# Rows and results in Pool's order at the start of the second experts

## The chip, the cores and the metric

One NeuronCore of one Trainium2 chip runs the whole program in one launch. The metric is the device time of that launch in microseconds. Engines are called PE (TensorE), DVE (VectorE), ACT (ScalarE), Pool (GpSimd) and SP (SyncE); L12 is line 12 of the kernel before.

## The reference

`x` holds 128 graphs of 64 nodes with 128 features, 8192 tokens in all, and runs through four residual stages. The change touches the seam between the last two:

```
x = x + gnn0(layernorm(x), adj)       # graph attention
x = x + ffn0(layernorm(x))            # 8 experts, top 2, relu
x = x + gnn1(layernorm(x), adj)       # three GRU layers on each graph
x = x + ffn1(layernorm(x))            # 16 experts, top 2

# ffn1, for every token
logits = x @ gate_w + gate_b
top_probs, top_idx = top_k(softmax(logits), 2)
hidden = silu(x @ w1[e]) * (x @ w2[e])
out = sum over the two experts e of top_prob[e] * (hidden @ w3[e])
```

All of it is computed in float32; the counting of ranks in the routing uses bfloat16 zeros and ones.

## The kernel before

The tokens are cut into 16 groups (`NG`) of 4 tiles of 128 tokens. The two expert stages compute only what is routed. For each group and each of the two chosen experts, a token has a slot in a queue in HBM (`queue1`), in which the tokens of an expert lie together. A *row send* is one indirect DMA that Pool issues at L429: it scatters 128 normalised tokens with their ids to their slots; a group needs TOPK * G = 8 of them (`queue_rows`). Group s uses buffer s % 4 of `c.rows` and the four semaphores `c.landed[s % 4]`.

The experts then read the queue in 144 tiles, two at a time, in 72 *pairs*. Which tiles can be known before the last groups are counted, the first `KNOWN` = 80 tiles or 40 pairs, come first; a table of the rest is written later. The function `experts` with layer = 1 is this stage. A step k of it does for each engine what belongs to three pairs at once (`steps`, `body`):

- SP loads the pair's tiles into `xq` (4 buffers), after the ids of four pairs before have been copied out.
- PE turns pair k (`ps_x`, L2326), does the up matmuls of pair k - 2 (16 of 128 x 128 into `e_ps_h`, two buffers, L2338) and the down matmuls of pair k - 4 (8, into `e_ps_y`, L2352).
- DVE copies pair k's ids into `y_ids` (8 buffers, L2432), copies the two experts' up weights into `e_up_of` (L2434), and multiplies the gate into `e_hT` for pair k - 2 (L2486). Ahead of the ids copy it waits until the results of pair k - 8, which used the same buffer, have landed.
- ACT copies the turned pair, does the silu (`e_gate`, L2409) and copies the results of pair k - 4 into `y_rows` (L2413).
- Pool sends the results of pair k - 4: two indirect DMAs at L2291 that scatter 128 results each to HBM. The first waits for `y_copied`. The second also waits for `h_made`, the up matmuls of the pair three further on.

The order on each engine is written by hand. Work of the stage before, on its last groups, is put between the steps by `between(k)`, called after step k: the statistics, the routing and the rows of groups 14 and 15 (`last`), and DVE's table of the remaining tiles behind steps 12 to 15. Groups 12 and 13 (`even`, `odd`) are ready as the stage begins: Pool sends their last 12 rows in front of its steps, with `rstd_and_shift` of groups 14 and 15 (L294, L296) among them. The rows of group 14 are sent all at once behind Pool's step 5, those of group 15 behind step 7.

Steps 0 to 15 (two rounds of `UNROLL` = 8) are straight code, steps 16 to 39 and the later ones are loops on the engine.

The results' first halves (t = 0) count on `c.landed[0]` and `c.landed[1]` (L2200), which groups 12 and 13 (s % 4 = 0 and 1) count on as well; the second halves count on `c.sent`. So Pool waits, ahead of its steps, until the rows of groups 12 and 13 have landed. SP waits ahead of pair 40 for the rows of groups 14 and 15.

Behind the last pair follows `finish`: SP loads the results back, ACT and DVE weight them and add them to `x`, SP stores `out`.

## Time and profile before

| what | value |
|---|---|
| median of three runs | 1069.83 us (1068.66 to 1069.91) |
| the profiled execution's own time | 1068.49 us |
| its span in the trace | 1066.8 us |
| PE busy | 950.5 us, 89% |
| DVE busy | 765.3 us, 72% |
| Pool busy | 589.0 us, 55% |
| ACT busy | 553.6 us, 52% |

The second experts take about the last quarter of the span. In the page's 40 slices of 26.7 us, PE's row reads 9 in nearly all slices and lower in those around 780 to 850 us, where one stage passes into the next. A timeline has one line for an instruction or a run of like ones: start, length, engine, line, operation and, in brackets, how long the engine had been idle and what ended that. A list of waits sums these. Windows give busy times of a stretch with the clock granted to PE (1.00 is 2.4 GHz, 0.50 is 1.2 GHz).

### The profile page before, as it was taken

The numbers are of one execution on the slowest core, as the hardware profiler recorded it, in microseconds if no ns is written. First come the engines' busy times: TensorE is split into PE (matmuls) and PEld (weight loads), VectorE is DVE, ScalarE is ACT, GpSimd is POOL, SyncE is SP. The second block draws the span as 40 slices with busy tenths as digits, with TensorE's granted clock in tenths as the row PEclk, the third lists the DMA queues.
The fourth block names the chain that finished last, engine by engine and source line by source line (L and its number), as shares of the span: only waits on it lengthen the run. The fifth ranks groups of instructions, "written<-read, shape, count | busy, mean of one in ns | idle before, by whom it ended". The sixth has DMA issues, their size and how long they took to land. (4 is left out here: it accounts for less than half of the span.)

```text
span 1066.8 us, 24109 instructions
## 1 busy us (share of the span) xinstructions
PE 950.5 (89%) x6368; PEld 772.8 (72%) x6369; DVE 765.3 (72%) x2973; ACT 553.6 (52%) x1359; POOL 589.0 (55%) x623
## 2 busy tenths in 40 slices
PE   4676999999999996899999999999969499999960
PEld 3566999999989996456555555555559499999960
DVE  5567888888876665478898899988866265555548
ACT  4655655665553342355576565655544144444455
POOL 2155677777777754001446455554546777676660
PEclk9656999999999999899999999999989799999985
DMA  9612422222222422210303303130115244333359
GB/s 225 225 38 59 103 76 83 76 79 75 76 83 74 123 66 82 80 53 27 97 23 109 100 26 107 35 122 26 36 45 116 67 116 119 86 94 92 86 206 313
DMA packets 101516, 99.41 MB, mean 93 GB/s; under 512 B 32412, under 2 KB 86300, under 8 KB 101148
## 3 DMA queue, kind: packets, MB, share of 16 engines
q1 hardware_dynamic: 84252, 62.83, 21.6%
q0 software_dynamic: 17152, 35.29, 9.9%
q8 instruction: 46, 0.75, 0.3%
q14 instruction: 66, 0.54, 0.2%
HBM read 55.44 MB, written 42.62 MB: 92 GB/s over the span
## 5 line engine op out<-in xcount | busy, mean ns | idle before, releaser
L429 POOL DMA_INDIRECT queue<-rows,slots x256 | 258.1, 1008 | 161.5 <-issue 72.5
L2291 POOL DMA_INDIRECT result<-y_rows,y_ids x144 | 143.3, 995 | 62.5 <-issue 52.6
L1015 POOL DMA_INDIRECT result<-y_rows,y_ids x136 | 134.8, 991 | 62.6 <-issue 36.1
L2338 PE MATMUL e_ps_h<-e_xT,e_up_of 128*128 128x128 f32 x1152 | 146.2, 282 | 15.3 <-DVE e_hT L2486 15.3
L2338 PEld LDWEIGHTS e_ps_h<-e_xT,e_up_of 128*128 128x128 f32 x1152 | 139.6, 198 | 16.0 <-issue 15.8
L1562 PEld LDWEIGHTS a_ps_y<-w_sb,a_hT 128*128 128x128 f32 x1088 | 131.2, 192 | 4.1 <-issue 1.3
L1562 PE MATMUL a_ps_y<-w_sb,a_hT 128*128 x1088 | 132.6, 275 | 1.1 <-DVE y_rows L1174 1.1
L1546 PE MATMUL a_ps_up<-a_xT,a_up_of 128*128 128x256 f32 x448 | 106.8, 381 | 0.3 <-issue 0.3
L2486 DVE TENSOR_TENSOR e_hT<-e_ps_h,e_gate 128x512 f32<-128x512 f32 x72 | 49.6, 689 | 72.4 <-ACT e_gate L2409 72.1
L2409 ACT ACTIVATE e_gate<-e_ps_h 128x512 f32<-128x512 f32 x72 | 43.0, 597 | 109.5 <-PE e_ps_h L2338 109.5
L1546 PEld LDWEIGHTS a_ps_up<-a_xT,a_up_of 128*128 128x128 f32 x448 | 80.7, 190 | 10.6 <-issue 0.5
L2014 ACT ACTIVATE g_rg<-g_ps_r,g_bsum 128x512 f32<-128x512 f32 x48 | 32.9, 685 | 92.8 <-PE g_ps_n L1931 92.8
L2352 PE MATMUL e_ps_y<-w_sb,e_hT 128*128 x576 | 78.5, 281 | 1.8 <-ACT y_rows L2413 1.8
L1374 ACT ACTIVATE a_hT<-a_ps_up,b_sb 128x256 f32<-128x256 f32 (+1 forms) x160 | 60.2, 436 | 35.0 <-PE a_ps_up L1546 23.4
L294 POOL TENSOR_TENSOR head_rstd<-head_vare,half_neg 128x4 f32<-128x4 f32 x15 | 15.7, 1046 | 107.5 <-DVE head_vare L287 107.5
L2352 PEld LDWEIGHTS e_ps_y<-w_sb,e_hT 128*128 128x128 f32 x576 | 72.3, 197 | 2.1 <-issue 2.1
L2434 DVE COPY e_up_of<-w_sb 128x512 f32 x144 | 60.2, 457 | 1.3 <-issue 0.4
L1155 DVE TENSOR_SCALAR a_hT<-a_ps_up,b_sb 128x256 f32<-128x256 f32 x112 | 48.9, 477 | 7.9 <-PE a_ps_up L1546 7.0
L1366 ACT ACTIVATE a_xT<-a_ps_x 128x256 f32<-128x256 f32 x68 | 25.8, 379 | 54.7 <-PE a_ps_x L1533 54.7
L2083 DVE SCALAR_TENSOR_TENSOR g_cand<-g_ps_hn,b_hh_sb,g_rg 128x512 f32<-128x512 f32 x48 | 35.8, 745 | 20.2 <-ACT g_rg L2014 19.9
L1924 PE MATMUL g_ps_r<-g_state,w_hh_sb 128*128 128x512 f32 x96 | 49.4, 596 | 0.0
L1929 PE MATMUL g_ps_r<-g_agg,w_agg 128*128 128x512 f32 x96 | 49.0, 592 | 0.0
(307 smaller groups left out, 2069.1 us busy)
## 6 DMA issues: line engine op xcount, KB each, us to landing
xq<-queue SPq DMA_DIRECT2D x168, 64.5 KB
g_y<-result SPq DMA_DIRECT2D x20, 512.0 KB, 4.3
xq<-queue SPq DMA_DIRECT2D x56, 129.0 KB
result<-y_rows,y_ids POOLq DMA_INDIRECT x280, 2.3
x_res<-x SPq DMA_DIRECT2D x16, 256.0 KB, 3.9
w_sb<-w SPq DMA_DIRECT2D x2, 2048.0 KB, 11.7
queue<-rows,slots POOLq DMA_INDIRECT x256, 2.4
w_sb<-w SPq DMA_DIRECT2D x16, 256.0 KB, 4.1
```

Of the source, the lines that this page charges most:

```text
L429: pool.indirect_dma_start(out=queue, out_offset=bass.IndirectOffsetOnAxis(ap=c.slots[q][:, k, t:t + 1], axis=0), in_=c.rows[q][:, k, t, :] ...
L1015: pool.indirect_dma_start(out=c.result0, out_offset=bass.IndirectOffsetOnAxis(ap=ids[slot.k][:, t, :].bitcast(U32), axis=0), in_=y[slot.k] ...
L1374: last = act.activation(hT[slot.b][:, q * size:(q + 1) * size], ps_up[0][:, q * size:(q + 1) * size], ACT.Relu, bias=up_b[:, bass.ds(exper ...
L1546: last = pe.matmul(ps_up[half][:, q * DOUBLE:(q + 1) * DOUBLE], up_of[b][:, (2 * half + q) * P:(2 * half + q + 1) * P], xT[b][:], start=Tr ...
L1562: last = pe.matmul(ps_y[:, t * D:(t + 1) * D], hT[at_down.b][:, first:first + P], down[:, bass.ds(expert_of(at_down, t) * wide + q * P, P) ...
L1924: pe.matmul(ps_r[:], c.w_hh[:, 0:D], h[:], start=True, stop=False)
L1929: pe.matmul(ps_r[:], c.w_agg[:, l, 0:D], agg[b][:], start=False, stop=True)
L2291: pool.indirect_dma_start(out=result, out_offset=bass.IndirectOffsetOnAxis(ap=ids[at_down.k][:, t, :].bitcast(U32), axis=0), in_=y[at_down ...
L2338: last = pe.matmul(ps_h[b][:, t, q * P:(q + 1) * P], up_of[at_up.k % 4][:, t, q * P:(q + 1) * P], xT[at_up.k % 4][:, t, :], start=True, st ...
L2352: last = pe.matmul(ps_y[:, t * D:(t + 1) * D], hT[at_down.k % 4][:, t, q * P:(q + 1) * P], down[:, bass.ds(e * (chunks * P) + q * P, P)], ...
L2434: last = v.tensor_copy(up_of[now.k % 4][:, t, :], up[:, bass.ds(expert_of(0, t) * wide, wide)])
L2486: v.tensor_tensor(hT[at_up.k % 4][:], ps_h[at_up.k % 2][:, :, H1:2 * H1], gate[at_up.k % 2][:], ALU.mult).then_inc(hT_vec, 1)
```

## The change

The results' first halves count on `c.sent_first`, eight semaphores that the first experts use and the rows don't. Pool no longer waits for the rows of groups 12 and 13; SP waits for them ahead of pair 40, with the others. The 16 rows of groups 14 and 15 are sent one at a time: `rows_by` spreads them over 24 steps, two for every three, behind the results of steps 6, 7, 9, 10 and so on to 28. For this all 40 steps with known tiles are straight code on Pool; the other engines keep their two rounds and their loops. And of the 12 rows in front of the steps three instead of two come before the first `rstd_and_shift`.

```diff
-        sent = [[c.landed[k // SPREAD][k % SPREAD] for k in range(UNROLL)], c.sent]
-        before = [[c.landed_before[k // SPREAD][k % SPREAD] for k in range(UNROLL)], c.sent_before[:]]
+        sent = [c.sent_first, c.sent]
+        before = [c.first_sent[:], c.sent_before[:]]
...
-            for i in range(2):
+            for i in range(rounds):
                 for k in range(UNROLL):
                     step(i, k)
                     if between:
                         between(i * UNROLL + k)
-            with eng.Fori(2, known // UNROLL) as i:
-                for k in range(UNROLL):
-                    step(i, k)
+            if rounds < known // UNROLL:
+                with eng.Fori(rounds, known // UNROLL) as i:
+                    for k in range(UNROLL):
+                        step(i, k)
...
                     for q in range(TURN):
-                        if q >= 2:
-                            wait_landed(sp, c, q, 0)
+                        wait_landed(sp, c, q, 0)
...
+            each_group = TOPK * G
+            shared_slots = 24
+            rows_by = [min(max(k - 5, 0) * PAIR * each_group // shared_slots, PAIR * each_group) for k in range(known + 1)]
+
             def between(k):
-                if k == 5:
-                    rows_of(last[0])
-                if k == 7:
-                    rows_of(last[1])
+                for row in range(rows_by[k], rows_by[k + 1]):
+                    rows_of(last[row // each_group], row % each_group, row % each_group + 1)
 
             even, odd = (At(NG // 2 - 2, b) for b in range(2))
-            rows_of(even, 4, 6)
+            rows_of(even, 4, 7)
             rstd_and_shift(pool, c, tail.norm, tail.VT, tail.GT, tail.AT0, last[0])
-            rows_of(even, 6, 8)
+            rows_of(even, 7, 8)
             rows_of(odd, 0, 2)
             rstd_and_shift(pool, c, tail.norm, tail.VT, tail.GT, tail.AT0, last[1])
             rows_of(odd, 2, 8)
-            for q in range(2):
-                wait_landed(pool, c, q, 0)
-            steps(pool, body, between=between)
+            steps(pool, body, between=between, rounds=known // UNROLL)
```

Pool's order at the start of the second experts, before (`queue` are row sends, `result` are result sends, two to a pair; x4 means four in a row):

```order
-L429 DMA queue<-rows,slots 135168x129 x2
-L294 TENSOR_TENSOR l_tail_rstd<-l_tail_vare,half_neg 128x4
-L296 TENSOR_TENSOR l_tail_shift<-l_tail_minus_mean,l_tail_rstd 128x4
-L429 DMA queue<-rows,slots 135168x129 x4
-L294 TENSOR_TENSOR l_tail_rstd<-l_tail_vare,half_neg 128x4
-L296 TENSOR_TENSOR l_tail_shift<-l_tail_minus_mean,l_tail_rstd 128x4
-L429 DMA queue<-rows,slots 135168x129 x6
-L2291 DMA result<-y_rows,y_ids 20480x128 x4
-L429 DMA queue<-rows,slots 135168x129 x8
-L2291 DMA result<-y_rows,y_ids 20480x128 x4
-L429 DMA queue<-rows,slots 135168x129 x8
-L2291 DMA result<-y_rows,y_ids 20480x128 x16
```

And now:

```order
+L429 DMA queue<-rows,slots 135168x129 x3
+L294 TENSOR_TENSOR l_tail_rstd<-l_tail_vare,half_neg 128x4
+L296 TENSOR_TENSOR l_tail_shift<-l_tail_minus_mean,l_tail_rstd 128x4
+L429 DMA queue<-rows,slots 135168x129 x3
+L294 TENSOR_TENSOR l_tail_rstd<-l_tail_vare,half_neg 128x4
+L296 TENSOR_TENSOR l_tail_shift<-l_tail_minus_mean,l_tail_rstd 128x4
+L429 DMA queue<-rows,slots 135168x129 x6
+L2291 DMA result<-y_rows,y_ids 20480x128 x6
+L429 DMA queue<-rows,slots 135168x129
+L2291 DMA result<-y_rows,y_ids 20480x128 x2
+L429 DMA queue<-rows,slots 135168x129
+L2291 DMA result<-y_rows,y_ids 20480x128 x4
```

The 16 row sends of groups 14 and 15 stood in two runs of eight, behind pair 1 and behind pair 3; now one stands behind pair 2 (six results), one behind pair 3, one behind pair 5, and so on. One row has moved ahead of the first `rstd`.

SP's order ahead of the load of pair 40, with its waits:

```order
 L600 ISA
 L600 DMA xq<-queue 128x129
-L590 TENSOR_LOAD tile_row [waits landed2_3,landed3_0,landed2_2,landed3_1,landed2_1,landed3_2,landed2_0,landed3_3,t1_written,t1_padded]
+L590 TENSOR_LOAD tile_row [waits landed1_3,landed2_0,landed1_2,landed2_1,landed1_1,landed2_2,landed1_0,landed2_3,landed0_3,landed3_0,landed0_2,landed3_1,landed0_1,landed3_2,landed0_0,landed3_3,t1_written,t1_padded]
 L600 ISA [waits e1_ids_copied]
 L600 DMA xq<-queue 128x129
```

The semaphores of buffers 0 and 1 (groups 12 and 13) have joined those of 2 and 3. No instruction of SP, PE, ACT or DVE has moved otherwise.

## Rows read from the trace of the kernel before

**Rows 1.** The page: the span, and PE's busy time and share.
```profile
span 1066.8 us, 24109 instructions
...
PE 950.5 (89%) x6368; PEld 772.8 (72%) x6369; DVE 765.3 (72%) x2973; ACT 553.6 (52%) x1359; POOL 589.0 (55%) x623
```

**Rows 2.** Waits, 795 to 870 us: engine, line, releaser; total, times, longest in us.
```profile
DVE y_ids L2432 <- DMA result<-y_rows,y_ids: 24.9, 5, 10.7
...
PE e_ps_h L2338 <- DVE e_hT L2486: 15.3, 2, 7.8
```

**Rows 3.** Timeline of PE: start, length, line, operation, count, [idle before it <- releaser].
```profile
822.91 1.95 PE L2338 MATMUL e_ps_h<-e_xT,e_up_of 128*128 128x128 f32 x16
...
836.66 3.58 PE L2338 MATMUL e_ps_h<-e_xT,e_up_of 128*128 128x128 f32 x16 [7.79 <-DVE e_hT L2486]
...
841.19 1.95 PE L2338 MATMUL e_ps_h<-e_xT,e_up_of 128*128 128x128 f32 x16
...
851.81 3.76 PE L2338 MATMUL e_ps_h<-e_xT,e_up_of 128*128 128x128 f32 x16 [7.56 <-DVE e_hT L2486]
...
857.25 1.95 PE L2338 MATMUL e_ps_h<-e_xT,e_up_of 128*128 128x128 f32 x16
...
915.36 1.95 PE L2338 MATMUL e_ps_h<-e_xT,e_up_of 128*128 128x128 f32 x16
```

**Rows 4.** Windows of 5 us: length, PE busy, granted PEclk, DMA share, GB/s.
```profile
825.00:830.00 5.00, 3.87 (x35) 1.00 0.21 65
835.00:840.00 5.00, 3.34 (x16) 0.51 0.35 97
```

**Rows 5.** Timeline of Pool, from the last rows of group 13 on.
```profile
809.77 0.95 POOL L429 DMA_INDIRECT queue<-rows,slots  x1 [0.30 <-issue]
814.82 0.96 POOL L2291 DMA_INDIRECT result<-y_rows,y_ids  x1 [4.09 <-issue]
817.46 0.96 POOL L2291 DMA_INDIRECT result<-y_rows,y_ids  x1 [1.69 <-ACT y_rows L2413]
...
830.07 0.96 POOL L429 DMA_INDIRECT queue<-rows,slots  x1 [0.30 <-issue]
831.34 0.96 POOL L2291 DMA_INDIRECT result<-y_rows,y_ids  x1 [0.31 <-issue]
832.60 0.96 POOL L2291 DMA_INDIRECT result<-y_rows,y_ids  x1 [0.30 <-issue]
...
847.75 0.96 POOL L2291 DMA_INDIRECT result<-y_rows,y_ids  x1 [0.30 <-issue]
```

**Rows 6.** Timeline of DVE behind the first long wait.
```profile
834.95 0.17 DVE L2432 COPY y_ids<-xq 128x2 f32<-128x2 f32 x1 [10.68 <-DMA result<-y_rows,y_ids]
...
835.83 0.68 DVE L2486 TENSOR_TENSOR e_hT<-e_ps_h,e_gate 128x512 f32<-128x512 f32 x1
```

**Rows 7.** Pool: a window (length, busy, count, PE's clock, DMA), and its longest distance.
```profile
863.10:890.50 27.40, 20.93 (x21) 1.00 0.45 124
...
869.73 1.19 POOL L2291 DMA_INDIRECT result<-y_rows,y_ids  x1 [0.30 <-issue]
871.22 0.95 POOL L2291 DMA_INDIRECT result<-y_rows,y_ids  x1 [0.30 <-issue]
```

**Rows 8.** Timeline at the stage's start: Pool's two rstd, ACT's first results.
```profile
793.85 1.27 POOL L294 TENSOR_TENSOR l_tail_rstd<-l_tail_vare,half_neg 128x4 f32<-128x4 f32 x1 [1.59 <-DVE l_tail_vare L287]
...
801.25 1.11 POOL L294 TENSOR_TENSOR l_tail_rstd<-l_tail_vare,half_neg 128x4 f32<-128x4 f32 x1
...
805.05 0.43 ACT L2413 ACTIVATE y_rows<-e_ps_y 128x128 f32<-128x128 f32 x2
```

**Rows 9.** Tile `queue`, Pool, 785 to 860 us: who waited for its sends (us, times).
```profile
  POOL result L2291: 4.1, 1
```

**Rows 10.** Timeline of ACT: its last results, at the stage's end.
```profile
1032.94 0.45 ACT L2413 ACTIVATE y_rows<-e_ps_y 128x128 f32<-128x128 f32 x2 [2.47 <-PE e_ps_y L2352]
```

**Rows 11.** Line L2434, 863 to 890 us: least, median, most ns of one.
```profile
L2434 DVE COPY e_up_of<-w_sb x21: 407/427/658, 863.3 to 889.7; 128x512 f32 x21
```

More of the change, by code:

```diff
@@ L2199, in experts, with steps @@
         y_made, y_copied = sem("y_made"), sem("y_copied")
-        sent = [[c.landed[k // SPREAD][k % SPREAD] for k in range(UNROLL)], c.sent]
-        before = [[c.landed_before[k // SPREAD][k % SPREAD] for k in range(UNROLL)], c.sent_before[:]]
+        sent = [c.sent_first, c.sent]
+        before = [c.first_sent[:], c.sent_before[:]]
         sent_of = [16 * (pairs // UNROLL + (k < pairs % UNROLL)) for k in range(UNROLL)]
-        def steps(eng, body, first_word=0, words=0, between=None):
+        def steps(eng, body, first_word=0, words=0, between=None, rounds=2):
             held = []
@@ L2293, in body, with rows_of @@
                             in_=y[at_down.k][:, t, :], in_offset=None).then_inc(sent[t][at_down.k], 16)
-            def rows_of(at, first=0, most=TOPK * G):
+            def rows_of(at, first, most):
                 wait(pool, tail.VK, "slots", at.s)
@@ L2494, in _ @@
                 finish.sum(v)
-    for k in range(UNROLL):
-        c.landed_before[k // SPREAD][k % SPREAD] += sent_of[k]
-        c.sent_before[k] += sent_of[k]
 def combine(v, c, y, t, k, g):
```

## The prediction

> **What bounds the kernel now.** I read the page first: PE is busy 950.5 of 1066.8 us [rows 1], so a change in the second experts pays only where PE stands still there. The list of waits for 795 to 870 us names one cause [rows 2]: DVE waited five times, 24.9 us in all, for result transfers to land before it could reuse a slot's ids buffer (L2432), and PE waited twice, 15.3 us in all, for DVE's `e_hT` behind that. Call U(p) the time at which PE starts the up matmuls of pair p (L2338). The timeline gives U(8) = 822.91, U(10) = 836.66, U(11) = 841.19, U(12) = 851.81, U(13) = 857.25 and U(33) = 915.36 [rows 3]. From U(13) to U(33) are 20 pairs in 58.1 us, 2.90 us each: PE without a break, at its own pace. From U(8) to U(33) are 25 pairs in 92.45 us, where 25 x 2.90 = 72.5: 20 us are lost. They lie in the steps to U(10) (13.75 instead of 5.8), U(11) (4.53), U(12) (10.62) and U(13) (5.44, each instead of 2.9): 8.0 + 1.6 + 7.7 + 2.5 = 19.8. The 1.6 and the 2.5 are matmuls at a lower clock after each stop: the 16 up matmuls take 3.58 and 3.76 us instead of 1.95 [rows 3], and the granted clock of 835 to 840 us is 0.51, the 1.2 GHz level [rows 4].
>
> Pool's timeline tells why [rows 5]. Pool sends the results of pairs 0 and 1, then eight rows of group 14 up to 830.07, then pair 2 at 831.34 and 832.60. The rows of group 15 stand in the same way between pairs 3 and 4; pair 4's second result goes at 847.75. Pair p+8 needs pair p's landing. From the start of pair 2's second result to U(10) are 4.06 us, from pair 4's to U(12) 4.06 us again. In it lie the landing (DVE's copy starts 2.35 us after), the two up copies and the product [rows 6]. So **U(p+8) = start of pair p's second result + 4.06**, or U(p+7) + 2.90, whichever is later.
>
> **The change, part by part.**
>
> *Removed bursts.* With no eight rows in front of any pair both stops go, with the slow matmuls behind them: up to 20 us. What is late next has to be worked out, since the 16 rows don't vanish: they are spread as two rows per three slots, behind pairs 2, 3, 5, 6 and so on to 23 and 24.
>
> *Pool's own pace.* With DVE mostly waiting, Pool made 13 starts from 831.34 to 847.75 [rows 5], 1.262 us from start to start. With PE and DVE at full pace, from 863.1 to 890.5 us, it made 21 in 27.4 us, 1.30 [rows 7]. The second fits the new stretch, since DVE will be working; I take 1.30 and keep 1.262 as the good end. A slot needs 2 + 2/3 sends: 3.47 us against PE's 2.90. Over the 24 slots Pool needs 13.6 us more than PE. It starts with a lead; that is used up, and then PE waits for Pool.
>
> *Where Pool starts.* Now it waits for the landing of groups 12 and 13, whose semaphores the results share: the last row goes at 809.77, the first result at 814.82, after 4.09 us of idle time, and the second at 817.46 after 1.69 us more [rows 5]; one result send waited 4.1 us for a row send [rows 9]. With semaphores of their own the results need only `y_rows`, which ACT has written for pair 0 at 805.05 [rows 8]. The third row ahead of the first `rstd` fits in Pool's 1.59 us of waiting for `vare` [rows 8], and one row less then stands ahead of the second `rstd`: it comes about 1.26 us earlier than 801.25, and so does ACT's normalising behind it. The last of the twelve rows thus starts near 808.5 and pair 0's first result near 809.8. The 1.69 us has no cause that the trace shows: its row names an ACT copy, but by the order of ACT's copies that is pair 3's, and this result waits for pair 0's; if it stays, the start counts as 811.5. This is the other end that I keep.
>
> *The sum.* Pair 2's second result, five starts on, goes at 816.3, and PE at its own pace would need it at 822.91 + 5.8 - 4.06 = 824.65: the lead is 8.3 us. From the first result to the second of pair 25 are 51 starts of results and 16 of rows, 67 in all. 809.8 + 67 x 1.30 = 896.9; plus 4.06 is U(33) = 901.0. Pair 25 is the right one to ask, as the last with all 16 rows in front; behind it Pool needs 2.60 us per pair and PE sets the pace again. PE alone would be at 822.91 + 72.5 = 895.4, so it waits about 5.6 us in all, in pieces of 0.7 to 1.0 us over the last ten or so of the pairs up to 33. Before, U(33) was 915.36. **The gain is 14.4 us.** The ends: 67 x 1.262 gives 898.4, a gain of 17.0; with the 1.69 us it is 902.7, a gain of 12.7.
>
> *Hidden parts, at nothing.* SP waits before pair 40 for all rows, also those of groups 12 and 13. The last row starts at 809.8 + 65 x 1.30 = 894.3 and has landed by 896.7; SP gets there only after DVE has copied the ids of pair 36, just ahead of U(34), near 903.7. That is 7 us of cover; a row landing later than that would delay the load of pair 40, and the loads queued behind it on SP, one for one. Queued behind the new rows on Pool are only results, which the sum holds. Pool runs 24 more slots as straight code instead of a loop: it does without the register work of the loop, and the 16 straight slots of before ran on at 1.26 us. PE's and ACT's orders don't change. The 1.26 us by which the second `rstd` comes earlier shortens a PE wait early on, but Pool sets U(33), not PE, so it is worth nothing.
>
> *From U(33) to the end* both kernels are alike: PE at 2.90 us per pair, then ACT's last results, which wait for PE [rows 10], and the finish behind them. So the gain reaches the end whole. The profiled run took 1068.49 us, its span was 1066.8; it would be 1054.1. The median of three is 1.3 us above it, and from that I forecast 1069.83 - 14.4 = **1055.4 us**.
>
> **A rule weighed.** Pool's send of 0.96 us became up to 1.19 us where DVE worked, with 1.49 us between two starts at worst [rows 7], and the mean rose by only 0.04 us. The Trainium skill, "SBUF — State Buffer", section "Who interferes with whom", says that a DVE copy in a 2-port mode and GpSimd exclude each other for a whole instruction, so that descriptors of a Pool transfer can't be written meanwhile. By that rule the change would be worse than its count of sends, as it puts more sends beside running copies; the trace agrees with a small effect at most. What full exclusion gives, worked out from rows, is the last rival below.
>
> **The rivals.**
>
> *Pool starts no earlier* (the change doesn't do what its semaphores are for). If the 4.09 us was not the landing, the first result is at 813.5 or so: 813.5 + 67 x 1.262 to 1.30 + 4.06 is U(33) = 902.1 to 904.7, a gain of 10.7 to 13.3: 1056.5 to 1059.1 us. For it speaks the unexplained 1.69 us beside it; against it [rows 9], though the timeline has only "issue" for it. 12%.
>
> *The clock falls in the short waits.* A fall cost 1.6 or 2.5 us in the two stops. Once PE is late by this it no longer waits for Pool until Pool has used up the time again, so falls don't add up: one lies on the path, so the gain is 14.4 or 12.7 less 1.6 to 2.5 us, 10.2 to 12.8: 1057.0 to 1059.6 us. Against it: from 825 to 830 PE was busy 3.87 of 5 us and was granted 1.00, the 2.4 GHz level [rows 4]. 8%.
>
> *Pool isn't in the way.* If its lead lasts, PE sets the pace: gain 20, 1049.9 us. That needs less than 1.22 us from start to start, which no stretch of sends has. 4%.
>
> *Pool starves, and the kernel is slower.* DVE's two up copies of a slot take 0.427 us each at full pace [rows 11]. If each held Pool for its whole time, 24 slots add 24 x 0.854 = 20.5 us to 64 sends, so 1.262 + 0.32 = 1.58 us from start to start: U(33) = 809.8 + 105.9 + 4.06 = 919.8, slower by 4.4, 1074.2 us. It decides from 1.515 us on, where 67 sends eat the whole gain; at the worst single distance of 1.49 the gain is 1.7 us. Against it: 21 sends in a row beside full DVE work took 1.30. 5%, split between a small gain, nothing, and slower.
>
> **How the numbers follow.** The forecast case (gain 12.7 to 17.0) has 71%, the rivals 12, 8, 4 and 5. The range reaches from the good end, 1052.8 less the 0.8 us or so between runs, 1052.0, to the bad end of the first two rivals, 1060.0. About 0.2% (2 us) is what a measurement of this kernel can tell from no change; all cases but the starved Pool are beyond it on the fast side: faster 0.95, same 0.02, slower 0.03.
>
> **What would show it.** In the changed profile: the first result near 809.8 (811.5 if the odd gap stays); rows single between results; the row of PE's waits for `e_hT` with 5 us in short pieces instead of 15.3 us in two, and all of them late; DVE's waits for landings in the same slots; U(33) near 901; granted clock 1.00 from 830 to 1000 us; 1.30 us between Pool's starts. The forecast fails if Pool's distance passes 1.33 us (each 0.03 us is 2 us), or if another transfer, such as the load of pair 40, ends later than a result.

## The result and the profile after

| | before | changed |
|---|---|---|
| median of four runs each, same chip | 1069.31 us (1068.66 to 1069.91) | 1052.2 us (1051.91 to 1053.0) |
| the profiled execution, its span | 1068.49, 1066.8 us | 1051.91, 1050.2 us |

The changed kernel takes 0.9841 of the time before (95% interval 0.9824 to 0.9858), 17.1 us less. The forecast was 1055.4 us, a gain of 14.4; the profiled executions differ by 16.6. On the third chip of the experiments below it took 1052.37 us beside 1069.65, a ratio of 0.9848 (0.9828 to 0.9867).

The page of the changed kernel, its first two lines, answers to [rows 1]. PE makes as many matmuls as before in 16.6 us less; it is busy 6.3 us less, having fewer matmuls at the lower clock:

```profile
span 1050.2 us, 24044 instructions
...
PE 944.2 (90%) x6368; PEld 764.4 (73%) x6369; DVE 764.9 (73%) x2973; ACT 554.1 (53%) x1359; POOL 589.1 (56%) x623
```

The list of waits, 795 to 905 us (who waited for what: us in total, times, longest), answers to [rows 2]:

```profile
DVE y_ids L2432 <- DMA result<-y_rows,y_ids: 31.2, 19, 4.4
...
PE e_ps_h L2338 <- DVE e_hT L2486: 4.8, 7, 1.1
```

DVE waits longer in all than before, but in 19 pieces, and PE's 15.3 us in two stops have become 4.8 us in seven pieces of at most 1.1 us.

PE's timeline answers to [rows 3] (start, length, line, operation; in brackets the idle time and what ended it). These are the up matmuls of pairs 8, 18, 33 and 71:

```profile
820.04 1.95 PE L2338 MATMUL e_ps_h<-e_xT,e_up_of 128*128 128x128 f32 x16
...
850.27 2.02 PE L2338 MATMUL e_ps_h<-e_xT,e_up_of 128*128 128x128 f32 x16 [1.08 <-DVE e_hT L2486]
...
899.61 1.58 PE L2338 MATMUL e_ps_h<-e_xT,e_up_of 128*128 128x128 f32 x12
...
1009.43 1.95 PE L2338 MATMUL e_ps_h<-e_xT,e_up_of 128*128 128x128 f32 x16
```

From U(8) to U(17) PE keeps its 2.90 us per pair; the first up matmuls behind a wait are pair 18's. U(33) is at 899.61, where 901.0 was forecast and 915.36 was before.

Windows of PE (stretch, its length, busy time, granted clock, DMA share, GB/s) answer to [rows 4]:

```profile
825.00:850.00 25.00, 24.19 (x218) 1.00 0.35 98
850.00:900.00 50.00, 45.87 (x393) 1.00 0.41 109
900.00:1000.00 100.00, 100.00 (x899) 1.00 0.34 95
```

The clock stays at its 2.4 GHz level through the short waits. Pool's timeline answers to [rows 5]: the last of the twelve rows, the results of pairs 0 to 2 without a gap (three of the six are shown), the first row of group 14, and 76 us later the last row of group 15 and pair 25's results:

```profile
807.86 0.95 POOL L429 DMA_INDIRECT queue<-rows,slots  x1 [0.30 <-issue]
809.12 0.96 POOL L2291 DMA_INDIRECT result<-y_rows,y_ids  x1 [0.30 <-issue]
810.38 0.95 POOL L2291 DMA_INDIRECT result<-y_rows,y_ids  x1 [0.31 <-issue]
...
815.44 0.96 POOL L2291 DMA_INDIRECT result<-y_rows,y_ids  x1 [0.31 <-issue]
816.70 0.96 POOL L429 DMA_INDIRECT queue<-rows,slots  x1 [0.30 <-issue]
...
892.87 0.96 POOL L429 DMA_INDIRECT queue<-rows,slots  x1 [0.30 <-ACT y_rows L2413]
894.13 0.96 POOL L2291 DMA_INDIRECT result<-y_rows,y_ids  x1 [0.31 <-issue]
895.40 0.96 POOL L2291 DMA_INDIRECT result<-y_rows,y_ids  x1 [0.30 <-issue]
```

**Where the 16.6 us are.** Up to U(33) 915.36 - 899.61 = 15.75. From U(33) to U(71) both kernels take 109.8 us. From U(71) to ACT's last results behind the last down matmuls, before took 1032.94 - 1025.17 = 7.77 us and the changed kernel 1016.38 - 1009.43 = 6.95: 0.8 more. Behind that both take 33.8 or 33.9 us. The 0.8 us is a matter of clock. These are PE's last down matmuls and ACT's last results, first of before, then of the changed kernel:

```profile
1030.94 1.97 PE L2352 MATMUL e_ps_y<-w_sb,e_hT 128*128 x8 [0.95 <-ACT y_rows L2413]
```

```profile
1015.19 1.15 PE L2352 MATMUL e_ps_y<-w_sb,e_hT 128*128 x8 [0.95 <-ACT y_rows L2413]
```

```profile
1016.38 0.45 ACT L2413 ACTIVATE y_rows<-e_ps_y 128x128 f32<-128x128 f32 x2 [1.66 <-PE e_ps_y L2352]
```

Same work, same wait of 0.95 us in front, 1.97 us against 1.15. Windows of PE over these matmuls, of before and of the changed kernel:

```profile
1031.00:1033.00 2.00, 1.91 (x8) 0.52 1.03 404
```

```profile
1015.00:1017.00 2.00, 1.15 (x8) 1.00 1.02 401
```

Before was granted 0.52, the 1.2 GHz level, the changed kernel 1.00. No instruction of the change is there. But the slow last matmuls are in the other kernel below that sends its rows in bursts as well (own semaphores alone: 2.00 us, and 41.6 us from U(71) to the end of the span, as in before), and in none of the eleven profiles without bursts (40.8 us). So it may be chance, or it may follow from the bursts; no run tells which.

### The profile page after: what moved, and what is told of

Read it like the earlier page. It is cut to its first block and busy times, and to the rows that moved or that the text cites. A ratio compares the mean times of both kernels' runs of the same rounds, so it can differ in the third digit from the quotient of the medians.

```text
span 1050.2 us, 24044 instructions
## 1 busy us (share of the span) xinstructions
PE 944.2 (90%) x6368; PEld 764.4 (73%) x6369; DVE 764.9 (73%) x2973; ACT 554.1 (53%) x1359; POOL 589.1 (56%) x623
## 5 line engine op out<-in xcount | busy, mean ns | idle before, releaser
L2338 PE MATMUL e_ps_h<-e_xT,e_up_of 128*128 128x128 f32 x1152 | 142.4, 277 | 4.9 <-DVE e_hT L2486 4.8
L2338 PEld LDWEIGHTS e_ps_h<-e_xT,e_up_of 128*128 128x128 f32 x1152 | 135.6, 193 | 6.9 <-DVE e_hT L2486 3.0
L2352 PE MATMUL e_ps_y<-w_sb,e_hT 128*128 x576 | 76.3, 275 | 1.8 <-ACT y_rows L2413 1.8
L2352 PEld LDWEIGHTS e_ps_y<-w_sb,e_hT 128*128 128x128 f32 x576 | 70.1, 192 | 2.1 <-issue 2.1
L2434 DVE COPY e_up_of<-w_sb 128x512 f32 x144 | 60.1, 457 | 2.5 <-issue 0.2
## 6 DMA issues: line engine op xcount, KB each, us to landing
w_sb<-w SPq DMA_DIRECT2D x2, 2048.0 KB, 12.6
```

The costliest lines, as they stand in the source:

```text
L2338: last = pe.matmul(ps_h[b][:, t, q * P:(q + 1) * P], up_of[at_up.k % 4][:, t, q * P:(q + 1) * P], xT[at_up.k % 4][:, t, :], start=True, st ...
L2352: last = pe.matmul(ps_y[:, t * D:(t + 1) * D], hT[at_down.k % 4][:, t, q * P:(q + 1) * P], down[:, bass.ds(e * (chunks * P) + q * P, P)], ...
L2434: last = v.tensor_copy(up_of[now.k % 4][:, t, :], up[:, bass.ds(expert_of(0, t) * wide, wide)])
```

## Experiments

Where the program before the second experts ends varies: Pool's first row send of this stage starts between 789.4 and 792.0 us in the profiled executions of all kernels here. So times inside the stage are given as distances from that send (789.42 in the changed kernel, 789.92 in before), where the changed kernel on two chips differs by 0.07 us at U(33). "First" and "second" are pair 0's two result sends, "pair 2" is pair 2's second result. "Less than before" is the median beside the before run on the same chip (1069.31, 1068.65, 1069.55 or 1069.65 us).

| kernel | first, second | pair 2 | U(8) | U(33) | U(37) | median, us | less than before | ratio (95%) |
|---|---|---|---|---|---|---|---|---|
| before | 24.89, 27.54 | 42.68 | 32.99 | 125.43 | 137.03 | | | |
| changed | 19.70, 20.96 | 26.02 | 30.62 | 110.19 | 121.86 | 1052.20 | 17.1 | .9841 (.9824 to .9858) |
| changed, third chip | 19.64, 20.90 | 25.97 | 30.57 | 110.12 | 121.79 | 1052.37 | 17.3 | .9848 (.9828 to .9867) |
| own semaphores alone | 19.66, 20.93 | 36.18 | 30.58 | 118.83 | 130.42 | 1062.13 | 6.5 | .9928 (.9909 to .9948) |
| spread rows alone | 25.89, 28.53 | 33.59 | 32.60 | 117.61 | 129.28 | 1061.87 | 6.8 | .9940 (.9924 to .9955) |
| 12 slots | 19.67, 20.93 | 27.25 | 30.59 | 114.33 | 125.92 | 1057.79 | 10.9 | .9903 (.9888 to .9918) |
| 28 slots | 19.68, 21.23 | 26.28 | 30.75 | 107.52 | 120.86 | 1052.17 | 16.5 | .9846 (.9831 to .9860) |
| two rows first | 21.15, 22.41 | 27.45 | 31.93 | 111.51 | 123.18 | 1052.57 | 17.0 | .9841 (.9822 to .9860) |
| four rows early | 15.10, 18.89 | 24.19 | 30.58 | 109.22 | 120.88 | 1051.57 | 18.0 | .9832 (.9815 to .9848) |
| four early, 28 slots | 15.09, 18.88 | 25.41 | 30.57 | 106.26 | 118.84 | 1050.25 | 19.3 | .9817 (.9798 to .9835) |
| the same, third chip | 15.11, 18.89 | 25.43 | 30.58 | 106.05 | 119.01 | 1050.36 | 19.3 | .9826 (.9806 to .9846) |
| two early, 28 slots | 17.12, 18.88 | 25.42 | 30.57 | 106.56 | 119.02 | 1050.81 | 18.8 | .9829 (.9809 to .9849) |
| up copies as maximum | 19.47, 20.73 | 26.68 | 30.90 | 113.98 | 125.65 | 1055.73 | 13.8 | .9868 (.9848 to .9888) |

### The two halves of the change

*Own semaphores alone*: the rows of groups 14 and 15 go in bursts of eight behind steps 5 and 7, as before, and Pool keeps its loop from step 16 on. The third row ahead of the first `rstd` stays.

```diff
             def between(k):
-                for row in range(rows_by[k], rows_by[k + 1]):
-                    rows_of(last[row // each_group], row % each_group, row % each_group + 1)
+                if k == 5:
+                    rows_of(last[0], 0, 8)
+                if k == 7:
+                    rows_of(last[1], 0, 8)
...
-            steps(pool, body, between=between, rounds=known // UNROLL)
+            steps(pool, body, between=between)
```

> One half of the change: results have semaphores of their own (and three rows stand ahead of the first rstd), but the rows of groups 14 and 15 go in two bursts of eight as before. Theory A (Pool's order of sends sets PE through U(p+8) = second result of pair p + 4.1 to 4.2 us): the first result starts at 809.1 as in the changed kernel, eight rows follow pair 1, pair 2's second result goes near 825.5 and PE's up 10 starts near 829.6 after a stop of about 4 us; eight more rows, pair 4's second result near 840.6, up 12 near 844.7 after a stop of about 9 us, then PE runs at 2.90 us per pair, with one or two slow steps: U(33) between 905.6 and 908, against 899.6 in the changed kernel and 915.4 before. Time about 1061 us (1059.5 to 1063.5), 8 us below before. Rival B (the bursts do all the harm, an earlier start is worth nothing): 1069, as before. Rival C (the wait for landed rows was the whole harm): 1052 to 1053.

PE's timeline of this kernel, the up matmuls of pairs 10 and 12:

```profile
830.58 3.52 PE L2336 MATMUL e_ps_h<-e_xT,e_up_of 128*128 128x128 f32 x16 [3.71 <-DVE e_hT L2484]
...
845.74 3.75 PE L2336 MATMUL e_ps_h<-e_xT,e_up_of 128*128 128x128 f32 x16 [7.63 <-DVE e_hT L2484]
```

Pool's timeline, the second results of pairs 2 and 4:

```profile
826.51 0.96 POOL L2291 DMA_INDIRECT result<-y_rows,y_ids  x1 [0.30 <-issue]
...
841.68 0.96 POOL L2291 DMA_INDIRECT result<-y_rows,y_ids  x1 [0.30 <-issue]
```

Both stops are still there; the matmuls behind them start 4.07 and 4.06 us behind their send and run at the lower clock. The whole burst pattern has moved: pair 2's second result is 6.50 us earlier than before, and U(33) 6.60. Up matmuls 10 and 12 come where they were expected; U(33) is 8.6 us behind the changed kernel's, a little beyond the expected 6 to 8.4.

*Spread rows alone*: the results count on the rows' semaphores again, and Pool, no longer SP, waits for the landing, ahead of its steps. The third row ahead of the first `rstd` stays here too.

```diff
-        sent = [c.sent_first, c.sent]
-        before = [c.first_sent[:], c.sent_before[:]]
+        sent = [[c.landed[k // SPREAD][k % SPREAD] for k in range(UNROLL)], c.sent]
+        before = [[c.landed_before[k // SPREAD][k % SPREAD] for k in range(UNROLL)], c.sent_before[:]]
...
+            for q in range(2):
+                wait_landed(pool, c, q, 0)
             steps(pool, body, between=between, rounds=known // UNROLL)
```

> The other half: rows spread over 24 slots as in the change, but results share semaphores with the rows of groups 12 and 13, so Pool waits for these rows to land ahead of its steps. Theory A: Pool's last early row starts at 807.9, the first result at about 813, 4 us later than in the changed kernel, and since Pool sets PE's time up to U(33), all of that reaches the end: U(33) about 903.6, time 1056 us. If the odd 1.69 us between the first and second result comes from the same wait, it is here again and the time is 1058 us; if it came from something else it is absent. Rival B (spreading is all, the lead covers the later start): 1052 to 1052.5, no difference from the changed kernel.

Pool's timeline of this kernel, the last row and the first two results:

```profile
810.29 0.96 POOL L429 DMA_INDIRECT queue<-rows,slots  x1 [0.30 <-issue]
817.78 0.96 POOL L2292 DMA_INDIRECT result<-y_rows,y_ids  x1 [6.54 <-issue]
820.42 0.96 POOL L2292 DMA_INDIRECT result<-y_rows,y_ids  x1 [1.69 <-ACT y_rows L2416]
```

The gain is 7.8 us at U(33), 3.4 less than the 11.2 expected with the stage's start taken out, and the miss is in the first two results. The wait for the landing was 7.49 us from the last row's start, where before it was 5.05 [rows 5]. The last row went 1.45 us earlier in the stage than before, and yet the first result came 1.00 us later.

The traces show what filled the DMA engines meanwhile. 10.7 us behind the stage's start, in before and here, SP issues one write of padding to the queue, 1032 KB (a step that no kernel here changes). First the issue in before, in SP's timeline and in the view of the DMA queues; then the queues' packets, of before from 803 to 806.5 us and with spread rows alone from 805 to 808.5 us (queue, kind: packets, MB, share of the 16 DMA engines):

```profile
800.57 1.22 SPq L578 DMA_DIRECT2D queue<-pad  x1
```

```profile
queue<-pad SPq DMA_DIRECT2D x1, 1032.0 KB
```

```profile
q1 hardware_dynamic: 1453, 0.75, 119.7%
```

```profile
q1 hardware_dynamic: 1409, 0.73, 115.7%
```

Pool's own queue (q0) is missing in the last two views: it moved no packet, though three of the twelve rows were sent in each stretch. In before its packets pause from 12.6 to 17.2 us behind the stage's start, with spread rows alone from 12.2 to 17.2, and their last one ahead of the first result ends at 22.2 and 22.8 us. So the length of this wait isn't a property of the twelve sends. That the padding is the cause isn't shown, since no run moved it, and the last 2.7 and 3.1 us up to the first result aren't explained.

From there the rule holds: 28.53 + 4.07 is U(8) = 32.60, and from the second result to pair 25's second are 84.9 us for 66 starts, 1.287 each, with U(33) 4.17 behind. The halves gain 6.6 and 7.8, together 14.4, against 15.2 for both. The stops and the late start are thus two losses, and most of each can be had alone. The sum is no clean one, since both halves contain the row moved ahead of the first `rstd` (1.3 us in the changed kernel, below).

### How many slots

*12 slots* and *28 slots* change one number:

```diff
-            shared_slots = 24
+            shared_slots = 12
```

> The changed kernel with its 16 rows spread over 12 slots instead of 24. Theory A: Pool is continuously busy in both, so the last pair behind all rows decides: pair 13, whose second result is 43 starts after the first, 809.1 + 43 x 1.288 + 4.2 = 868.7 = U(21), and from there 2.90 us per pair: U(33) = 903.5 against 899.6. Time 3.9 us above the changed kernel, 1056.1 us (1055 to 1058.5, the upper end if PE's clock falls in stops that are now up to 2 us long). Rival B (only bursts that outlast DVE's eight buffers hurt, four rows in three slots don't): 1052.2, or better since the rows are done sooner.

> The changed kernel with its 16 rows spread over 28 slots. Theory A: pair 29 decides, 75 starts after the first: 809.1 + 75 x 1.288 + 4.2 = 909.9 = U(37), where the changed kernel has 911.2: 1.3 us faster, 1050.9 us. The last row lands near 907, about 4.5 us after SP comes to its wait ahead of pair 40; the load of pair 40 is needed near 912, so this is still hidden. Rival D (SP's wait for the last row reaches PE): pair 40 comes late, U(38) is 2 us or more later than 2.90 us behind U(37), and the time is 1052 to 1055 us.

With 12 slots U(33) is 4.1 us later than in the changed kernel (3.9 expected), with 28 slots U(37) is 1.0 us earlier (1.3 expected). So the term "sends in front of the deciding pair, times Pool's distance" is right as a slope too. With 12 slots the single waits are longer, and one of them costs clock. PE's timeline of that kernel, its longest wait, and the window behind it:

```profile
848.99 2.27 PE L2338 MATMUL e_ps_h<-e_xT,e_up_of 128*128 128x128 f32 x15 [2.56 <-DVE e_hT L2486]
```

```profile
849.00:851.00 2.00, 2.00 (x15) 0.86 0.31 73
```

With 28 slots the time, 1052.17 us, can't be told from the changed kernel's; the 1050.9 expected didn't come. The rows are sent later, but pair 40 isn't late: U(71) is 219.08, also 0.9 earlier. The wait of SP is still hidden.

### Where Pool starts

*Two rows first* undoes the third row ahead of the first `rstd_and_shift`:

```diff
-            rows_of(even, 4, 7)
+            rows_of(even, 4, 6)
...
-            rows_of(even, 7, 8)
+            rows_of(even, 6, 8)
```

> The changed kernel with one edit undone: two rows, not three, ahead of the first rstd, so four ahead of the second. Theory A: Pool waits 1.6 us for vare again, the twelve early rows end one send later and the first result starts 21.0 us behind the stage's first row send instead of 19.7; Pool sets U(33), so U(33) is 1.3 us later too, 111.5 us behind the stage's first row send against 110.2 in the changed kernel. PE also stands still again for 1.4 us at about 803 us and runs some 5 us at the lower clock; that is hidden. Time about 1053.5 us. Rival (what the order of rows and rstd does is hidden): no difference in U(33).

The first result is 1.45 us later, U(8) 1.31 and U(33) 1.32. This part of the change is thus worth 1.3 us in the trace, all of it by Pool's start: that PE's U(8) comes earlier too counts for nothing, since Pool decides U(33). The medians (17.0 and 17.1 us less than before) don't show it, which is within their scatter.

*Four rows early* sends the last four rows of group 12 in the GRU stage, in gaps of Pool; *28 slots* comes on top in the next one, starting one step sooner:

```diff
-                    rows_of(even, 1, s_tok, u + 5)
-                    rows_of(even, 2, s_aggT, u + 5)
-                    rows_of(even, 3, s_r, u + 5)
+                    if n == pairs - 1:
+                        for m in range(1, 8):
+                            rows_of(even, m)
+                    else:
+                        rows_of(even, 1, s_tok, u + 5)
+                        rows_of(even, 2, s_aggT, u + 5)
+                        rows_of(even, 3, s_r, u + 5)
...
-            rows_of(even, 4, 7)
+            rows_of(odd, 0, 3)
             rstd_and_shift(pool, c, tail.norm, tail.VT, tail.GT, tail.AT0, last[0])
-            rows_of(even, 7, 8)
-            rows_of(odd, 0, 2)
+            rows_of(odd, 3, 6)
             rstd_and_shift(pool, c, tail.norm, tail.VT, tail.GT, tail.AT0, last[1])
-            rows_of(odd, 2, 8)
+            rows_of(odd, 6, 8)
```

```diff
-            shared_slots = 24
-            rows_by = [min(max(k - 5, 0) * PAIR * each_group // shared_slots, PAIR * each_group) for k in range(known + 1)]
+            shared_slots = 28
+            rows_by = [min(max(k - 4, 0) * PAIR * each_group // shared_slots, PAIR * each_group) for k in range(known + 1)]
```

> The changed kernel with the last four rows of group 12 sent in the GRU stage, right behind the first four and without the waits that paced those (Pool stood idle 2.3, 3.1 and 3.8 us there), so that eight rows instead of twelve stand ahead of the steps (three, rstd, three, rstd, two). Theory A: the first result is then held by ACT's y_rows and the second of pair 2 by PE's up matmuls of pair 5, at 812.9 in the changed kernel's time where it went at 815.4; all later sends are 2.5 us earlier, U(33) is 107.6 us behind the stage's first row send against 110.2. Time 1049.7 us. Rival: eight sends back to back beside the last GRU layer lengthen it (DVE's products there), and the stage begins 1 to 3 us later: 1051 to 1053 us.

> The early rows of the run above, and the 16 rows of groups 14 and 15 begin one slot sooner (behind pair 1, where Pool would wait) and are spread over 28 slots. Theory A: pair 28 decides, 67 starts behind pair 2's second result at 812.9: 812.9 + 67 x 1.288 + 4.15 = 903.3 = U(36), where the changed kernel has 908.4: 5 us faster, 1047.2 us, and PE waits only about 2 us for Pool in all. Rival: the last row lands too late for the load of pair 40, or the GRU stage is lengthened; then 1049 to 1052 us.

The first result did start 4.6 us earlier, but U(33) gained 1.0 us and U(37), with 28 slots, 3.0. Pool's timeline of the second kernel (its run on the third chip) around the first results:

```profile
805.28 0.96 POOL L429 DMA_INDIRECT queue<-rows,slots  x1 [0.30 <-issue]
807.05 0.96 POOL L2295 DMA_INDIRECT result<-y_rows,y_ids  x1 [0.81 <-ACT y_rows L2416]
810.83 0.96 POOL L2295 DMA_INDIRECT result<-y_rows,y_ids  x1 [2.82 <-issue]
```

The second result is held for 2.82 us, so more than half of what the first one won is lost. By the program it waits for pair 0's `y_rows` and for the up matmuls of pair 3. PE's and ACT's timelines of the same run show both:

```profile
806.03 1.95 PE L2341 MATMUL e_ps_h<-e_xT,e_up_of 128*128 128x128 f32 x16
```

```profile
805.91 0.43 ACT L2416 ACTIVATE y_rows<-e_ps_y 128x128 f32<-128x128 f32 x2
```

They end at 807.98 and 806.34. Even from the later of them 2.85 us are unexplained. The view of the DMA queues of this run for 806 to 811.5 us (queue, kind: packets, MB, share) lists data alone and no instruction queue, so it shows no loading of code:

```profile
q1 hardware_dynamic: 1817, 0.91, 98.4%
q0 software_dynamic: 91, 0.19, 17.3%
```

It also shows the DMA engines full: the hold lies in the same stretch, behind the write of padding, in which the rows landed late above. No run separates the two.

To tell whether the early rows or that hold matter, a kernel between the two was run, *two rows early, 28 slots* (six instead of eight of group 12 sent in the GRU stage), beside the changed kernel and *four early, 28 slots* once more, all on the third chip:

```diff
-                        for m in range(1, 8):
+                        for m in range(1, 6):
                             rows_of(even, m)
...
-            rows_of(odd, 0, 3)
+            rows_of(even, 6, 8)
+            rows_of(odd, 0, 1)
...
-            rows_of(odd, 3, 6)
+            rows_of(odd, 1, 4)
...
-            rows_of(odd, 6, 8)
+            rows_of(odd, 4, 8)
```

> The changed kernel as it is, on the chip of the next two runs, so that they can be compared with it. Expected: U(33) 110.2 us behind the stage's first row send, U(37) 121.9; 0.984 of the kernel before, some 1052.5 us.

> The kernel with four rows of group 12 in the GRU stage and 28 slots, again, beside the changed kernel. Its first look had U(37) 118.8 us behind the stage's first row send, 3.0 us less than the changed kernel, not 5, because Pool stood idle 2.8 us between the first two results. Expected: the same distances, and a time 3 us below the changed kernel's on the same chip, 1049.5 us.

> As the run above, but only two rows of group 12 more in the GRU stage (six there, ten ahead of the steps), so that Pool has rows left to send until pair 0's and 1's results are there. Theory A (Pool's uninterrupted sends set PE's time): no idle time between the first two results; pair 2's second result 24.7 us behind the stage's first row send instead of 25.4 with four rows, U(37) 0.7 us earlier, 118.1 us. Time 3.7 us below the changed kernel's, about 1049 us. Rival (early rows are worth their number): U(37) one to two sends later than with four, 120 to 121.4 us.

Pool's timeline of *two early, 28 slots*:

```profile
807.74 0.96 POOL L429 DMA_INDIRECT queue<-rows,slots  x1 [0.30 <-issue]
809.00 0.95 POOL L2295 DMA_INDIRECT result<-y_rows,y_ids  x1 [0.30 <-issue]
810.76 0.96 POOL L2295 DMA_INDIRECT result<-y_rows,y_ids  x1 [0.81 <-issue]
```

The first result is 2.0 us later than with four early, the second at the same 18.88 us behind the stage's start, and U(37) is 119.02 against 119.01. So the first result doesn't matter, what holds the second does, and it comes at a fixed time of the stage: more than two rows early buy nothing. Both expectations for this run missed, since each counted the early rows. What it is that comes at 18.9 us, the trace doesn't show, and it stays open; the padding's stretch, from 10.7 us on, is the rival that no run tested. The version with four early and 28 slots is the best of those run: 1050.25 and 1050.36 us, 2.0 us below the changed kernel on the third chip, where 3 were expected; the intervals of the two ratios there overlap, while U(71) is earlier by 2.7 us (217.21 against 219.94).

### Whether DVE holds Pool up

*Up copies as maximum*: DVE's two copies of up weights become a maximum of the weights with themselves, which gives the same values; it reads two inputs instead of one.

```diff
-                    last = v.tensor_copy(up_of[now.k % 4][:, t, :], up[:, bass.ds(expert_of(0, t) * wide, wide)])
+                    weights_of = up[:, bass.ds(expert_of(0, t) * wide, wide)]
+                    last = v.tensor_tensor(up_of[now.k % 4][:, t, :], weights_of, weights_of, ALU.max)
```

> The changed kernel with DVE's two copies of the up weights in each slot made as the maximum of the weights with themselves (a tensor_tensor of two SBUF operands, the same values), about 0.69 us instead of 0.43 each. Theory S (these copies hold up Pool's sends: 1.288 us from start to start beside them, 1.262 without): the distance falls to 1.263 us, the path from landing to up matmul grows by 0.5 us, and U(33) is 109.0 us behind the stage's first row send against 110.2: 1051 us. The Trainium skill, SBUF - State Buffer, section Who interferes with whom, has a copy in a 2-port mode exclude GpSimd and a tensor_tensor contend only with GpSimd's reads, which would be this case. Rival N (the 0.026 us comes from something else): distance 1.288, U(33) 0.5 us later, 1052.7 us. Rival R (two SBUF inputs hold up Pool more than the copies do): distance over 1.30, 1054 us or more.

Pool's sends between 820 and 895 us are busy 0.985 us in the mean in the changed kernel (58 of them) and 1.029 in this one (56). From start to start, from pair 0's second result to pair 25's, they are 1.288 and 1.341 us. Rival R of the expectation came in. One slot of the second kernel, DVE and then Pool:

```profile
851.40 1.29 DVE L2435 TENSOR_TENSOR e_up_of<-w_sb 128x512 f32 x2
```

```profile
850.86 0.96 POOL L429 DMA_INDIRECT queue<-rows,slots  x1 [0.31 <-issue]
852.12 1.41 POOL L2291 DMA_INDIRECT result<-y_rows,y_ids  x1 [0.30 <-issue]
853.83 0.97 POOL L2291 DMA_INDIRECT result<-y_rows,y_ids  x1 [0.30 <-issue]
```

Of the sends between 815 and 895 us, those that overlap an up copy took 1.007 us in the changed kernel (34 of them) and those that don't 0.957 (28); with the maximum it is 1.059 (44) and 0.958 (16). So DVE's work does hold sends up, by 0.05 us in the mean with the copy and 0.10 with the maximum. These means hide how. In the slot above the second maximum ends at 851.40 + 1.29 = 852.69, 0.57 us behind the start of the send at 852.12, and this send takes 1.41 us, 0.45 more than 0.957. The send at 850.86, inside which the first maximum begins, takes 0.96.

This repeats send by send. Take the sends that began at least 0.05 us behind the start of a copy or maximum and over 0.12 us ahead of its end: 11 of 62 in the changed kernel (1.093 us in the mean) and 23 of 60 with the maximum (1.151). Each is longer than 0.957 us by the time from 0.12 us behind its own start to the end of that DVE instruction, to 0.013 us. The others took 0.96 us in the mean in both kernels, among them six of the changed kernel that began within 0.04 us of a copy's start. So a send that begins while either instruction runs is held until it ends. The mean effect is small because few sends begin there, and it is greater with the maximum because that is longer (0.69 us against 0.43). The two maxima of a slot also take 0.5 us longer than the copies (1.29 against 0.77), which is the lag from pair 25's second result to U(33), 4.71 instead of 4.21. Together: 66 x 0.053 = 3.5 us, plus 0.5, less 0.2 of the start, is the 3.8 us by which U(33) is later.

## Why the prediction was right, point by point

**Pool's sends set U(33): right.** In the changed kernel it is 4.21 us behind pair 25's second result; 12 and 28 slots moved U(33) and U(37) by the sends added and taken away; a longer distance between sends moved it by 66 times the excess.

**The distance between sends, 1.30 us: 1.288.** The stretch of before [rows 7] gave a little too much, the change's 24 slots a little less: 0.8 us of the result. The good end, 1.262, is the distance behind a send that no up copy holds; the first six results kept it (809.12 to 815.44).

**The first result at 809.8: 809.12.** Of this 0.5 us is that the stage itself began at 789.42 instead of 789.92, which is no effect of the change; 0.2 us is size. That the odd 1.69 us gap would go was the choice made, and it went: the second result is 1.26 us behind the first. It is back in the kernel with spread rows alone, so it goes with Pool's wait for the landing. What it consists of stays open: the kernels with four rows early have a like hold without that wait.

**The lag, 4.06 us: 4.21.** It held to 0.01 us in stops, when DVE had nothing else to do (before, and own semaphores alone). At full pace DVE starts the up copies 0.28 us behind the ids copy's start, and the landing took 2.42. DVE's timeline of the changed kernel, the slot that U(33) waits for, answers to [rows 6]:

```profile
897.82 0.17 DVE L2432 COPY y_ids<-xq 128x2 f32<-128x2 f32 x1 [1.91 <-DMA result<-y_rows,y_ids]
898.10 0.77 DVE L2434 COPY e_up_of<-w_sb 128x512 f32 x2
898.78 0.69 DVE L2486 TENSOR_TENSOR e_hT<-e_ps_h,e_gate 128x512 f32<-128x512 f32 x1
```

**The end alike: 0.8 us off**, the clock in the last down matmuls shown above; the forecast put no term there. In sum: the forecast's 14.4, plus 0.5 (stage's start), 0.2 (first result), 0.8 (distance) and 0.8 (end), less 0.15 (lag), is 16.55, against 16.6 measured. Of this the 0.5 is scatter, the 0.8 at the end may be, and the forecast's own terms were mis-sized by 0.85.

The medians' gain, 17.1 us, lies 2.7 above the forecast: the 2.15 of these terms, and 0.5 because the profiled executions lie 0.8 below their median in before and 0.3 in the changed kernel. It is just beyond the good end of the forecast case (17.0), and 1052.2 us is at the very edge of the stated range (from 1052.0). So the mechanism is shown by the profiles, while that the time still fell inside the range owes something to luck.

**PE's waits, 5.6 us and all late: 7.1 us lost, from U(18) on.** U(8) to U(33) took 79.57 us instead of 72.5; the list of waits shows 4.8 us of it as idle, in pieces of 0.4 to 1.1. PE came to U(8) at 820.04, not 822.91: 0.5 us is the stage's start, and the rest came because with `rstd` earlier it neither stood still nor fell in clock around 804 us. PE's timeline around pair 3's up matmuls, of before:

```profile
804.46 0.66 PE L1687 MATMUL e_ps_m<-ident,rows 128*128 128x128 f32 x4 [1.43 <-ACT rows L303]
...
805.17 3.04 PE L2338 MATMUL e_ps_h<-e_xT,e_up_of 128*128 128x128 f32 x16
```

and of the changed kernel:

```profile
802.84 0.66 PE L1687 MATMUL e_ps_m<-ident,rows 128*128 128x128 f32 x4
...
803.55 1.95 PE L2338 MATMUL e_ps_h<-e_xT,e_up_of 128*128 128x128 f32 x16
```

PE's head start only made it wait sooner and longer for Pool. "Worth nothing on PE's side" was right, the size of the wait was not.

**SP's wait ahead of pair 40 hidden: right**, even with 28 slots.

**The rivals.** *Pool starts no earlier*: not so. The landing was what Pool waited for, and its price isn't even steady (5.05 us in before, 7.49 with spread rows alone). *The clock falls in short waits*: not here, with waits up to 1.1 us, nor with one of 1.47 us (two early, 28 slots: 1.00 throughout). In other kernels it did: behind a wait of 1.86 us (spread rows alone, the up matmuls of pair 8 took 3.41 us, granted 0.55) and behind one of 2.56 us (12 slots). The up matmuls of pair 8 with spread rows alone:

```profile
824.49 3.41 PE L2341 MATMUL e_ps_h<-e_xT,e_up_of 128*128 128x128 f32 x16 [1.86 <-DVE e_hT L2489]
```

*Pool isn't in the way*: it was.

*Pool starves*: the mechanism exists, at a small fraction of the price. The 24 slots' copies would have added 20.5 us if each held Pool for its whole time. Measured, a copy holds at most the one send that begins while it runs, and for the rest of its time only: the 62 sends between 815 and 895 us were 1.7 us longer in all than 62 x 0.957. The Trainium skill, "SBUF — State Buffer", section "Who interferes with whom", says that a 2-port copy and GpSimd shut each other out for a whole instruction, and that a `tensor_tensor` with two inputs in SBUF contends with GpSimd's reads only, from which it infers that the writing of descriptors is left alone. The trace agrees on the copy: each of the 11 sends caught by one was held to its end. It doesn't agree with the inference: the two-input maximum held a send to its end just the same (23 sends). There the measurement decides.

## What to carry to other kernels

When a slow serial engine sits between two fast ones, count its instructions from the first that is free to go to the last that somebody waits for, multiply by their distance, and compare with the fast engine's own pace: moving such work costs nothing until that sum is the longer, and each piece beyond it costs its full distance. An instruction that waits on a shared counter also waits for everybody else who counts on it, and how long it takes until DMAs have landed is not theirs alone to say (5.05 and 7.49 us for the same sends); semaphores of their own, with one row moved, took away 6.6 us. Ask not only how much a mean grows beside another engine's work, but which instructions grow and by how much: the means of 0.05 and 0.10 us above hid a hold of up to 0.47. Compare distances inside the stage: the program before it moved by 2.5 us between executions, more than several of the effects measured here.

## What the runs showed of the hardware

- An indirect DMA send by Pool (128 rows) is busy 0.957 us alone and 1.26 us from start to start. One that began while DVE ran a 128x512 float32 copy, or a maximum of two SBUF inputs of that size, was held until that instruction ended (1.093 us in the mean for 11 sends beside copies, 1.151 for 23 beside maxima, 1.43 at most). One inside which the copy or maximum began took 0.96 to 1.04.
- The wait for a burst of row sends to land, from the last one's start, was 5.05 us in one kernel and 7.49 in another with the same twelve rows in front. In both, Pool's DMA queue moved no packet for some 5 us, from 12 us behind the stage's start on, while the engines carried another queue's packets at a share of 115% and more, behind a write of 1032 KB.
- Pair 0's second result started 2.65 us behind the first wherever Pool had just waited for a landing (before, spread rows alone), and at 18.9 us behind the stage's start in all kernels whose first result was early, with an idle time that the trace gives to nothing. Its cause was not found.
